# A fused feed-forward, linear attention and feed-forward layer on 8 cores: casts tied to attention items, VectorE's order within an item, and where two transposes stand

## The reference

```python
def _L0_ffn_ref(x, w_gate, w_up, w_down):  
    gate = jnp.einsum('bsd,hd->bsh', x, wg)
    up = jnp.einsum('bsd,hd->bsh', x, wu)
    h = jax.nn.silu(gate) * up
    return jnp.einsum('bsh,dh->bsd', h, wd)

# attention: 16 heads of 64, 128 random features, causal
z = einsum('bhsd,md->bhsm', x, omega) - 0.5 * sum(x * x)
phi = exp(z - max(z)) / sqrt(128) + 1e-6
S_kv += kt[..., :, None] * vt[..., None, :];  s_k += kt
out_t = (qt @ S_kv) / (qt @ s_k + 1e-6)
attn = outs @ Wo
h = _layernorm(batch + attn, gamma, beta)
out = jnp.maximum(h @ W1 + b1, 0.0) @ W2 + b2

x = x + 0.5 * _L0_ffn_ref(_layernorm(x), w_gate, w_up, w_down)
x = x + _L0_attn_ref(_layernorm(x), ...)
x = x + 0.5 * _L0_ffn_ref(_layernorm(x), w_gate, w_up, w_down)
```

## Time and profile before

| | |
|---|---|
| median of 3 runs | 1794.32 us |
| profiled execution, its own time | 1797.32 us |
| its span on the slowest core (core 1) | 1795.7 us |
| spans of the 8 cores | 1781.7 to 1795.7 us |
| TensorE (PE) busy on core 1 | 1764.9 us, 98% of the span |
| VectorE (DVE) | 782.0 us, 44% |
| ScalarE (ACT) | 444.2 us, 25% |
| GpSimd (POOL) | 184.4 us, 10% |
| mean granted TensorE clock, core 1 | 0.996 |

### The profile page before, as it was taken

One profiled execution on the slowest core, in us unless ns is written; L12 is line 12 of the kernel. 1 busy time (PEld: TensorE's weight loads), 2 busy tenths in 40 slices (PEclk: granted clock), 3 DMA queues, 4 the chain that ended last, 5 costly groups with the idle time before them and its releaser, 6 DMA issues.

```text
span 1795.7 us, 29867 instructions; the slowest of 8 cores (1781.7 to 1795.7 us)
## 1 busy us (share of the span) xinstructions
PE 1764.9 (98%) x9312; PEld 839.6 (47%) x9312; DVE 782.0 (44%) x1697; ACT 444.2 (25%) x983; POOL 184.4 (10%) x355
## 2 busy tenths in 40 slices
PE   8999999999999979999999999999999999999999
PEld 4444444444455434444444444444544444444444
DVE  5344116511686334656465433567533110431331
ACT  3112002202554135322331430233241130110110
POOL 3011102100011011102001000101001100000000
PEclk9999999999999989999999999999999999999999
DMA  9999999999999587777555765746666564544543
GB/s 192 234 219 211 202 185 183 199 217 174 213 197 196 163 151 170 173 186 201 154 150 162 212 193 177 199 151 162 174 194 197 166 181 152 170 158 153 199 152 107
DMA packets 198903, 324.57 MB, mean 181 GB/s; under 512 B 125792, under 2 KB 125920, under 8 KB 198752
## 3 DMA queue, kind: packets, MB, share of 16 engines
q1 hardware_dynamic: 185936, 277.49, 54.2%
q0 software_dynamic: 12240, 44.11, 18.5%
q10 hardware_dynamic: 576, 1.05, 0.2%
HBM read 311.12 MB, written 52.43 MB: 202 GB/s over the span
## 4 chain that ended last, share of the span: by engine, by line
PE 93%; DMA 3%; DVE 1%; SPq 1%; issue 1%; ACT 0%; POOL 0%; DVEq 0%; ACTq 0%; POOLq 0%
PE d_ps L912 36%; PE d_ps L969 30%; PE d_ps L946 17%; PE a_ps L1059 2%; PE d_ps L1059 2%; DMA ring<-gu_b 2%; SPq L406 1%; DMA x_tm<-xin 1%; PE a_ps L563 1%; PE a_ps L465 1%; PE a_ps L466 1%; DMA ffm<-ftm 1%; PE a_ps L589 0%; PE a_ps L517 0%; PE a_ps L594 0%
## 5 line engine op out<-in xcount | busy, mean ns | idle before, releaser
L969 PE MATMUL d_ps<-ring,big 128*128 128x512 bf16 x2176 | 488.1, 380 | 0.0
L969 PEld LDWEIGHTS d_ps<-ring,big 128*128 128x128 bf16 x2176 | 207.5, 98 | 233.1 <-issue 1.9
L1123 ACT ACTIVATE th_t<-d_ps 128x512 f32<-128x512 f32 x192 | 114.9, 598 | 620.0 <-PE d_ps L912 616.7
L912 PE MATMUL d_ps<-fmX,ring 128*128 128x512 bf16 x1136 | 261.1, 379 | 3.9 <-DMA ring<-gu_b 3.9
L912 PE MATMUL d_ps<-fmZ,ring 128*128 128x512 bf16 x1152 | 255.7, 379 | 0.0
L1240 DVE SCALAR_TENSOR_TENSOR th_t<-th_t,d_ps 128x512 f32<-128x512 f32 x192 | 131.5, 685 | 210.7 <-ACT th_t L1123 210.2
L486 ACT ACTIVATE ftm<-a_ps,nmax 128x128 bf16<-128x128 f32 x512 | 146.4, 369 | 241.4 <-DVE nmax L473 230.7
L912 PE MATMUL d_ps<-fmY,ring 128*128 128x512 bf16 x768 | 169.7, 379 | 0.0
L912 PEld LDWEIGHTS d_ps<-fmZ,ring 128*128 128x128 bf16 x1152 | 110.7, 98 | 126.1
L912 PEld LDWEIGHTS d_ps<-fmX,ring 128*128 128x128 bf16 x1136 | 107.4, 98 | 120.8 <-issue 4.5
L946 PE MATMUL d_ps<-fmX,ring 128*128 128x512 bf16 x640 | 145.4, 382 | 10.8 <-ACT fmX L416 10.8
(11 more groups left out here) (88 smaller groups left out, 1399.0 us busy)
## 6 DMA issues: line engine op xcount, KB each, us to landing
ring<-gu_b SPq DMA_DIRECT2D x144, 512.0 KB, 4.2
ring<-w_b SPq DMA_DIRECT2D x128, 512.0 KB, 4.2
ring<-d_b SPq DMA_DIRECT2D x72, 512.0 KB, 4.9
w_b<-w_f POOLq DMA_DIRECT2D x32, 512.0 KB, 10.8
ring<-gu_i POOLq DMA_DIRECT2D x24, 512.0 KB, 12.7
gu_b<-ring SPq DMA_DIRECT2D x24, 512.0 KB, 22.1
ring<-q_b SPq DMA_DIRECT2D x16, 512.0 KB, 6.0
ring<-k_b SPq DMA_DIRECT2D x16, 512.0 KB, 3.9
```

Of the source, the lines that this page charges most:

```text
L912: r = e.matmul(d_ps[bank][:, :], ring[:, so + g * 1024 + k * 128:so + g * 1024 + (k + 1) * 128], xT[:, k * 512:(k + 1) * 512], start=(k == ...
L969: r = e.matmul(d_ps[t][:, :], lhs[:, o:o + 128], ring[:, so + i * 512:so + (i + 1) * 512], start=(s == 0 and i == 0), stop=(s == n_slots - ...
L1123: e.activation(th_t[:, (n % 2) * 512:(n % 2 + 1) * 512], d_ps[2 * (n % 2)][:, :], AF.Tanh, scale=TANH_SC).then_inc(s_tanh, 1)
```

## The change

Four edits:

1. In `pool_attn` every cast piece now waits for `s_pk`, so that it isn't issued before TensorE has projected item i of the block. Block 0 issues pieces up to its last steps (15 of them instead of 13); block 1 still issues 4.
2. In `pool_program` the pieces ahead of the attention are 29 instead of 31: 9 instead of 10 in the gated layer of block 2 and 4 instead of 5 in Q and K of block 0, at other counts.
3. In `dve_attn` the even step of blocks 1 to 3 has the scaling first, then the state, then the features. Block 0 keeps the features first, and has the scaling ahead of the state.
4. In the head the third and fourth transpose of block 1 move from tick 1 to ticks 2 and 3, on TensorE and on ScalarE, and one run of three zero matmuls goes.

```diff
--- before.py
+++ after.py
@@ -666,12 +666,15 @@
                 if 0 <= i - back < 32:
                     dve_mask(e, t0 + i - back)
             else:
-                if 0 <= i - 1 < 32:
+
+                if 0 <= i - 1 < 32 and b < FX_BLOCK:
                     dve_feat(e, t0 + i - 1)
+                if 0 <= i - back - 2 < 32:
+                    dve_tail(e, t0 + i - back - 2, t0 + min(i - 1, 32))
                 if 0 <= i - 2 < 32:
                     dve_state(e, t0 + i - 2)
-                if 0 <= i - back - 2 < 32:
-                    dve_tail(e, t0 + i - back - 2, t0 + min(i - 1, 32))
+                if 0 <= i - 1 < 32 and b >= FX_BLOCK:
+                    dve_feat(e, t0 + i - 1)
             if b < 3:
                 if s + 5 in LN_STEP:
                     dve_ln_stats(e, LN2, b + 1, LN_STEP.index(s + 5))
@@ -690,7 +693,9 @@
                 i = s // 2
                 if s % 2 == 0 and 0 <= i - 5 < 32 and (b < 3 or i - 5 < 24):
                     pool_state(e, 32 * b + i - 5)
-                if (b == 0 and s % 5 == 1 and s < 62) or (b == 1 and s % 5 == 1 and s < 20):
+                if s % 5 == 1 and (b == 0 or b == 1 and s < 20):
+
+                    e.wait_ge(s_pk, 32 * b + min(i + 1, 32))
                     cast_piece(e)
                 if b > 0 and s in (8, 16, 24, 32):
                     pool_b2(e, b - 1, s // 8 - 1)
@@ -863,14 +868,14 @@
                     pool_ln_rstd(e, LN2, 0, i // 2)
                 if i in (9, 11, 13, 15):
                     pool_ln_rstd(e, LN1, 3, (i - 9) // 2)
-                if i % 12 in (1, 3, 5, 8, 10):
+                if i % 8 in (1, 4, 6):
                     e.wait_ge(s_up, 48 + i)
                     cast_piece(e)
             for i in range(4):
                 e.wait_ge(s_d, 96 + 12 * i + 4)
                 cast_piece(e)
-            for i in range(5):
-                e.wait_ge(s_qk, 3 * i + 1)
+            for i in range(4):
+                e.wait_ge(s_qk, 4 * i + 1)
                 cast_piece(e)
             for b in range(NB):
                 pool_attn(e, b)
@@ -1023,10 +1028,12 @@
             def first(k):
                 if k == 1:
                     busy(16)
-                    for j in range(4):
-                        pe_ln_transpose(e, LN1, 1, j, j)
-                        if j < 3:
-                            busy(3)
+                    pe_ln_transpose(e, LN1, 1, 0, 0)
+                    busy(3)
+                    pe_ln_transpose(e, LN1, 1, 1, 1)
+                    busy(3)
+                if k in (2, 3):
+                    pe_ln_transpose(e, LN1, 1, k, k)
                 pe_ln_tick(e, LN1, 2, k, 48, 8, 5)
             side = Ticks(first)
             held = {}
@@ -1173,9 +1180,8 @@
             e.wait_ge(s_const, 48)
 
             def first(k):
-                if k == 1:
-                    for j in range(4):
-                        act_ln_evict(e, LN1, 1, j, j)
+                for j in ((), (0, 1), (2,), (3,))[k] if k < 4 else ():
+                    act_ln_evict(e, LN1, 1, j, j)
                 act_ln_tick(e, LN1, 2, k, 48, 8, 5)
             side = Ticks(first)
             for bb, i in first_pass:
```

## The result

The changed kernel takes 1772.46 us (median of 4 runs, from 1771.56); the kernel before, measured beside it, has 1793.05 and 1794.32 us. Some executions of any of these kernels fall into a slower state, in which one die shows a lower granted clock (1990.83 us here, 1839.41 and 2059.82 us for the kernel before), and the ratios and mean spans in this document leave them out. The ratio is 0.9876, with an interval from 0.9857 to 0.9896. The direction and the mechanism held; one term of the sum was far too small.

The account below looks back on a forecast made before the run. TensorE, busy 1764.9 of 1795.7 us, was taken as the bound, with only its idle time to win. Terms summed to -18.7 on core 1 (1777.0) and -11.8 on core 6 (1778.3, then last); forecast 1779 us, range 1773 to 1790.

Parts of the forecast that it names:

- Block 1's first two casts: Casts beside block 0's transposes of y: TensorE's gamma and beta wait goes, 10.8 us on core 1, plus 1.8 of clock.
- Block 0's first two casts: Three pieces issued together at 427 us: spreading them removes ring-load waits, 3.9 us on core 1, 2.2 on core 6.
- VectorE's order: Even attention steps: scaling runs within the wait for exponentials, gaining 3.2 us on core 1 and 4.3 on core 6.
- The output waits for the scaling, the delta behind it for features and state.: Even steps on VectorE: what TensorE's odd step was said to need from each operation; no size of its own.
- The last of the three still decides: Scaling, state and features on VectorE: only what stood idle ahead of the features can be won; bounds 0 and 5.2 us.
- New casts in block 1: Two more casts beside block 1's feature transposes: a cost of 0 to 4 us, taken as 1.
- The head: Second transpose pair earlier, third about unchanged: 0 on core 1, -1 to +1 us elsewhere, +0.5 on core 6.
- A: Block 0's transposes of y stay late behind ring loads; 1789 us; chance 0.12.
- B: New casts in block 1 cost 7.6 us instead of 1, with clock drops; 1785 to 1786 us; chance 0.12.
- C: Feature transposes beside casts become as slow as block 0's transposes, 14.3 us; 1805 us, slower than before; chance 0.04.
- D: Cast waits do little for all but four pieces; 1781 us if ring loads stay late; chance 0.70 together with the forecast.
- a gain beyond the sum: Whole kernel: a gain larger than the summed terms; chance 0.02.

Follow-up runs that it names:

- four_at_transposes: The kernel before with block 1's four cast pieces issued together at its first step; 1802.44 us in a single run.
- wait_block1_only: The kernel before with the cast pieces' wait on the projections in block 1 alone; 1793.84 us, ratio 0.9945.
- casts_only: The kernel before with only the cast pieces as in the changed kernel, VectorE's order and head as before; 1783.27 us, ratio 0.9891.
- after_old_head: The changed kernel with the head as before; 1771.63 us, ratio 0.9829 to the kernel before.
- after_feat_first: The changed kernel with features, then scaling, then state on VectorE in blocks 1 to 3; 1780.85 us, ratio 0.9927.
- state_last: The changed kernel with scaling, then features, then state on VectorE in blocks 1 to 3; 1772.31 us, ratio 0.9882.

## Why the prediction was wrong

- **Block 1's first two casts (-10.8 and -1.8 on core 1): right.** The earlier trace rows were the right model: 2.83 and 3.31 us for the transposes. Of the 15.5 us by which `w1(0)` begins earlier, 10.8 + 3.9 + 0.4 are this wait, the ring loads and the head. `four_at_transposes` and `wait_block1_only` show the cause.
- **Block 0's first two casts (-3.9): right.** No wait for `gu_b` is left, and in `wait_block1_only`, without that edit, it stays. On core 6 the clock fell behind this wait too (0.50 from 458 to 460 us), 1.7 us that the prediction has nowhere.
- **VectorE's order (-3.2 and -4.3): the step that failed.** The prediction had the mechanism: the scaling runs within the wait for exponentials, and all waits but the longest go. It sized the term by the matmuls' rows, 5.2 us in seven pieces. Measured are 10.4 to 10.7 us in the mean of the cores (`casts_only` to `after_old_head`), and about as much on core 1. Three things were missing. The waits cost what their loads list, nearly (9.2 + 0.9 for 5.2 on core 1). The longest wait shrank by 1.3 us where 0.3 were taken: its load was 2.46 us late and is 1.13 late now. 0.4 of that is the features and the state no longer ahead of the scaling; the rest is that VectorE begins the norm's row (L313) 1.93 us ahead of the load of L563 now, and 0.85 before. And the lower clock behind it, 1.7 us on this core, was put at nothing.
- **"The output waits for the scaling, the delta behind it for features and state."** The output waits for the state as well (L585). "The last of the three still decides" stands with this: in `after_feat_first` the last of them ends late and the gain is gone, in `state_last` and in the changed kernel it ends soon after the features.
- **New casts in block 1 (+1): about right.** 0 us on core 1, 1.9 on core 2, and 0 to 3.1 in the other versions. In the profiled executions of the changed kernel it is what picks the slowest core, core 2 both times; the prediction had core 6 there.
- **The head (0, +0.5 on core 6): right on core 1, too low on core 6.** The third pair begins 0.4 us earlier on core 1. On core 6 TensorE waits 1.5 us for the second ring slot and the pair begins at 35.08 us for 33.53, 1.55 later, outside the -1 to +1 given. In the mean of the cores it is 33.1 for 33.0. Without the edit the time is 1771.63 on another chip, so it is worth nothing that can be told.
- **Rivals.** A falls by the transposes' rows, B by waits of 0 to 1.9 us, C by all. D named the right places. What should have been a rival was a gain beyond the sum, to which the prediction gave 0.02.

On core 1: 10.8 + 1.8 + 3.9 + 10.5 + 0.4 and the 1.2 us for a feature transpose of the earlier trace rows, which didn't recur, make 28.6 of 29.2 us. On core 6, where the loads' rows shrink by 9.8 us: 5.0 + 1.7 + 2.2 + 1.7 + 9.8 + 1.7 - 1.55 make 20.6 of 20.8.

## What to carry to other kernels

Where a semaphore holds a matmul, compare the starts of the products ahead and behind with a place where nothing waits, or read the waits of its weight load and of the next one, not the matmul's: here they were nearly twice as large, and the measured gain followed them. Ahead of an in-order engine's operation that another engine waits for, put nothing that itself waits; look for the engine's own row of waits (93.6 us here), since the waits that others have for it come in pieces too small to list. Bulk DMAs that wait for nothing are worth a wait on progress when quick transposes stand beside them.

## What had not been expected

A wait of 2.3 us was enough for the granted clock to be at 0.50 from 774 to 776 us, 2 us behind its end. But the same wait, 2.3 to 2.4 us long, left it at 1.00 on four of the eight cores of the kernel before, on one of `casts_only` and on four of `after_feat_first`. No run here shows what decides it, so the 1.7 us of such a wait can't be counted on either way. And the price of a slow DMA grows with what is queued on the other queue: four transposes took 5.9 to 7.2 us beside no cast, 13.5 to 21.4 beside two and 24.0 to 27.9 beside four.
